# First attention phase: query/key parts and bf16 copies placed by DMA through DRAM instead of by selection matmuls and masked copies

## What is computed

```python
x = x + attn_a(layernorm(x))          # x: 16 sequences x 512 tokens x 256
qkv = xn @ w_qkv + b_qkv              # 16 heads of 16
scores = einsum('bhqd,bhkd->bhqk', q, k) * 16 ** -0.5
scores = where(mask, -inf, scores)    # heads 0-3: causal; heads 4-15: causal and a window of 64 keys
ctx = softmax(scores) @ v
x = x + ctx @ w_out + b_out
```

## Time and profile before

| | us |
|---|---|
| median of three executions | 3148.2 |
| profiled execution, span | 3151.3 |
| phase a, from the first instruction to its last store's issue | 1045.4 |
| busy in the whole span: PE, DVE, ACT, POOL | 2820.9, 2193.1, 1499.6, 1419.0 |

### The profile page before, as it was taken

How to read it: one execution, slowest core, us unless ns; L and a number is a source line. 1 busy time by engine, 2 the same in 40 slices (tenths; PEclk the granted TensorE clock), 3 DMA queues, 4 the chain that set the end, 5 groups by cost and what they waited for, 6 DMA issues and landing times. The chain is left out here.

```text
span 3151.3 us, 59461 instructions
## 1 busy us (share of the span) xinstructions
PE 2820.9 (90%) x17856; PEld 2175.0 (69%) x17856; DVE 2193.1 (70%) x5372; ACT 1499.6 (48%) x3002; POOL 1419.0 (45%) x1606
## 2 busy tenths in 40 slices
PE   6999999998999688898997999999999949999993
PEld 4565655565655457787896787778787739888872
DVE  8887787778886487765565676867777655566664
ACT  3455444454455234555775443344343317666651
POOL 1332233323333173446632533457575535655556
PEclk9999999999999788999998999999999979999996
DMA  4121111211211355657984222334343248888885
GB/s 151 48 89 49 49 55 70 68 49 56 73 58 49 134 190 178 220 195 268 324 291 145 86 76 71 99 112 127 111 127 105 96 156 300 289 304 302 299 277 155
DMA packets 208998, 465.15 MB, mean 148 GB/s; under 512 B 28448, under 2 KB 119712, under 8 KB 207648
## 3 DMA queue, kind: packets, MB, share of 16 engines
q1 hardware_dynamic: 159520, 326.86, 30.3%
q0 software_dynamic: 49152, 134.28, 12.8%
HBM read 217.24 MB, written 243.27 MB: 146 GB/s over the span
## 5 line engine op out<-in xcount | busy, mean ns | idle before, releaser
L381 POOL TENSOR_SCALAR_AFFINE_SELECT a_pt<-a_pt 128x512 f32<-128x512 f32 (+1 forms) x320 | 178.0, 556 | 669.5 <-ACT a_pt L481 668.8
L481 ACT ACTIVATE a_pt<-a_S 128x384 f32<-128x384 f32 (+3 forms) x640 | 254.6, 452 | 265.3 <-PE a_S L779 261.9
L1059 POOL DMA_INDIRECT slots<-f_xn,k_picks x256 | 260.0, 1016 | 254.2 <-PE f_Z L1567 99.7
L1842 POOL DMA_INDIRECT k_yg<-made,k_picks x224 | 223.6, 998 | 254.2 <-PE b_Y L2355 138.1
L2637 POOL DMA_INDIRECT f_yg<-made,k_picks x256 | 255.1, 997 | 170.8 <-PE f_Z L2830 89.7
L629 DVE TENSOR_REDUCE a_mx<-a_FB 128x2 f32<-128x384 f32 (+4 forms) x512 | 276.1, 591 | 26.7 <-PE a_FB L754 13.7
L751 PE MATMUL a_FB<-a_kb,a_qb 128*128 128x192 bf16 (+4 forms) x1024 | 206.1, 267 | 58.7 <-DVE a_mx L629 51.3
L1856 POOL DMA_INDIRECT slots<-b_staged,k_picks x160 | 162.3, 1015 | 105.9 <-issue 38.9
L792 PE MATMUL a_PV<-a_pt,a_vv 128*32 128x192 f32 (+4 forms) x2048 | 198.4, 371 | 2.7 <-POOL a_pt L388 2.6
L751 PEld LDWEIGHTS a_FB<-a_kb,a_qb 128*128 128x128 bf16 x1024 | 102.1, 100 | 135.1 <-DVE a_mx L629 87.0
L779 PE MATMUL a_S<-a_qs,a_ks 97*128 97x384 f32 (+3 forms) x640 | 178.3, 361 | 15.6 <-issue 15.3
(11 more groups left out here) (418 smaller groups left out, 7509.2 us busy)
## 6 DMA issues: line engine op xcount, KB each, us to landing
f_xg<-slots SPq DMA_DIRECT2D x164, 512.0 KB, 6.1
made<-f_ye SPq DMA_DIRECT2D x164, 512.0 KB, 4.0
slots<-a_zeros SPq DMA_DIRECT2D x16, 2560.0 KB, 9.2
a_xin<-in_x SPq DMA_DIRECT2D x16, 512.0 KB, 10.1
x_after_a<-a_xres SPq DMA_DIRECT2D x16, 512.0 KB, 2.9
f_wexp<-in_w_exp SPq DMA_DIRECT2D x8, 1024.0 KB, 13.4
k_xin<-bases SPq DMA_DIRECT2D x16, 512.0 KB, 5.7
x_after_b<-b_xres SPq DMA_DIRECT2D x16, 512.0 KB, 3.1
```

Source lines behind the costliest of these rows:

```text
L381: ins = nc.gpsimd.affine_select(out=v[:, :, 0:P], in_=v[:, :, 0:P], compare_op=ALU.is_ge, fill=0.0, base=0, pattern=[[0, nh], [1, P]], cha ...
L481: nc.scalar.activation(pt[:, u % 4, b * w:(b + 1) * w], S[:, s_bank[2 * u + b], 0:w], ACT.Exp).then_inc(e_done, 1)
L1059: nc.gpsimd.indirect_dma_start(out=slots[GROUP1[s]][:, :], out_offset=bass.IndirectOffsetOnAxis(ap=picks[:, i:i + 1], axis=0), in_=xn[:, s ...
L1842: nc.gpsimd.indirect_dma_start(out=yg[:, b, k, :], out_offset=None, in_=made[GROUP1[s]][:, :], in_offset=bass.IndirectOffsetOnAxis(ap=rout ...
```

## The change

The selection matrices, the rk and rq uses and the masks go. For each of two tiles t of 128 channels (8 heads), DVE makes bf16 copies `q16`, `k16` (`halve`, 4 casts of a sequence in slots 5 and 6). SP stores them to DRAM (`store_half`), waits until they have landed, and loads them back (`load_half`) with each head's 16 rows on partitions 0 to 15 of that head's place in `qb16` and `kb16`; the other partitions are zeroed once at the start. In the same way SP stores the four parts (`store_parts`) and loads them as nine DMAs for each t into `ks` and `qs` (`load_parts`). The factor 16^-0.5 moves into the exponential's scale. All front uses are now evicted by DVE in one count (`f_dve`), v and m move by a slot, mT by one, and `PE_FIRST` becomes (3, 4). The raw weights share memory with `pt`.

```diff
-    timed = ([(4, ("T", 0)), (4, ("T", 1)), (5, ("q", 0)), (6, ("k", 0)), (6, ("q", 1)), (6, ("k", 1)),
-              (10, ("v", 0)), (8, ("v", 1))] +
-             spread(9, 5.5, MAXG) + [(15, ("mT", 0))] + spread(13, 10.0, MAXL) + [(23, ("mT", 1))])
-    for p, slot in enumerate((15, 15, 16, 16, 18, 18, 21, 22)):
-        timed += [(slot, ("rk", p)), (slot, ("rq", p))]
+    timed = ([(4, ("T", 0)), (4, ("T", 1)), (5, ("q", 0)), (5, ("k", 0)), (6, ("q", 1)), (6, ("k", 1)),
+              (8, ("v", 0)), (9, ("v", 1))] +
+             spread(10, 6.0, MAXG) + [(16, ("mT", 0))] + spread(14, 10.0, MAXL) + [(24, ("mT", 1))])
...
-        PE_FIRST = (3, 7)
+        PE_FIRST = (3, 4)
-        MASK_AT = (5, 5, 8, 7)
-        K_AT = (6, 7)
+        HALF_AT = (5, 6)
...
+                def store_half(s, t):
+                    sp.wait_ge(halved, 2 * QT * s + 2 * (t + 1))
...
+                    for c, src in (("q", q16), ("k", k16)):
+                        sp.dma_start(half_d[c][s % 2, t * P:(t + 1) * P], src[:, t]).then_inc(half_stored[t], 16)
+
+                def load_half(s, t):
+                    sp.wait_ge(half_stored[t], 32 * (s + 1))
+                    if s:
+                        sp.wait_ge(f_done, ev(s - 1, NF, m_of[t]))
...
+                    for c, dst in (("q", qb16), ("k", kb16)):
+                        sp.dma_start(dst[0:DH, HT * t:HT * (t + 1), :],
+                                     half_d[c][s % 2, t * P:(t + 1) * P].rearrange("(h d) n -> d h n", d=DH)
+                                     ).then_inc(half_loaded[t], 16)
+
+                def store_parts(s, t):
+                    sp.wait_ge(f_dve, ev(s, NF, at["k", t]))
...
+                def load_parts(s, t):
+                    sp.wait_ge(parts_stored[t], 64 * (s + 1))
+                    if s:
+                        sp.wait_ge(s_done, ev(s - 1, 2 * NU, 2 * t_last[2 * t + 1] + 1))
...
+                    for n, i in enumerate((0, 0, 1)):
+                        sp.dma_start(ks[n * PAIR:(n + 1) * PAIR, PT * t:PT * (t + 1), :].bitcast(F32),
+                                     hilo_d["k"][s % 2, i, t * P:(t + 1) * P].rearrange("(a r) n -> r a n", r=PAIR)
+                                     ).then_inc(parts_loaded[t], 16)
+                    for n, i in enumerate((0, 1, 0)):
+                        for j in range(2):
+                            r = n * PAIR + j * DH
...
+                    if core:
+                        load_parts(s, 1)
                     if not isinstance(s, int) or 2 <= s + 2 < nseq:
                         load(s + 2, par)
                     if core:
                         m_rows(s, 1)
+                    if front:
+                        store_half(s + 1, 0)
+                        store_parts(s + 1, 0)
+                        store_half(s + 1, 1)
+                        load_half(s + 1, 0)
+                        store_parts(s + 1, 1)
+                        load_half(s + 1, 1)
                     if tail:
                         at_least(sp, t_dve, summed)
                         sp.dma_start(rows, xres[:, 1 - par]).then_inc(x_stored, 16)
                         at_least(sp, x_stored, stored)
                     if front:
+                        load_parts(s + 1, 0)
                         m_rows(s + 1, 0)
                         clear(s + 1)
...
-                def mask_q(s, four):
...
-                    for h in range(4 * four, 4 * four + 4):
-                        ins = nc.vector.tensor_scalar(qb16[:, h, :], qh[:, t, :].bitcast(F32),
-                                                      headmask[:, h % HT:h % HT + 1], None, ALU.mult)
...
+                def halve(s, t):
+                    at_least(dve, half_stored[t], ev(s - 1, 32, 31))
+                    for c, dst, src in (("q", q16, qh), ("k", k16, kh)):
+                        at_least(dve, hi_done, ev(s, NH, HIGH.index((c, t))))
+                        nc.vector.tensor_copy(dst[:, t, :], src[:, t, :].bitcast(F32)).then_inc(halved, 1)
...
+                nc.vector.memset(qs[0:ONES].bitcast(F32), 0.0).then_inc(dve_ready, 1)
...
-                    elif kind in ("rk", "rq"):
-                        c, t, a = kind[1], k // PT, k % PT
...
-                        pe.matmul(dst[0:ONES, :], sel[c + "h"][:, a].rearrange("p b c -> p (b c)"), hi[:, t, :],
-                                  start=True, stop=False)
-                        ins = pe.matmul(dst[0:ONES, :], sel[c + "l"][:, a].rearrange("p b c -> p (b c)"), lo[:, t, :],
-                                        start=False, stop=True)
                     elif kind == "m":
...
-                        at_least(pe, q_masked, ev(s, 4, heads[-1] // 4))
-                        at_least(pe, k_half, ev(s, QT, heads[-1] // HT))
+                        at_least(pe, half_loaded[heads[-1] // HT], ev(s, 32, 31))
```

More of the change, by code:

```diff
@@ L177, in phase_a @@
     s_bank, s_before = rotation(2 * NU, 3)
-    by_act = [kind == "rk" or (kind == "rq" and k in BY_ACT) for kind, k in FRONT]
-    act_no = [sum(by_act[:i]) for i in range(NF)]
-    dve_no = [i - act_no[i] for i in range(NF)]
-    NFA, NFD = sum(by_act), NF - sum(by_act)
     at = {use: i for i, use in enumerate(FRONT)}
     slot_front = {u: [i for i in range(NF) if timed[i][0] == u] for u in range(2 * NU)}
-    assert timed[-1][0] - NU < timed[0][0]
+    assert timed[-1][0] - NU <= timed[0][0]
     HIGH = [("T", 0), ("T", 1)] + [(c, t) for t in range(QT) for c in ("q", "k")]
@@ L242, in phase_a @@
         zeros = sb("zeros", [P, 4 * H])
+        hilo_d = {c: nc.dram_tensor("a_%s_parts" % c, (2, 2, H, SEQ), F32, kind="Internal").ap() for c in "qk"}
+        half_d = {c: nc.dram_tensor("a_%s_half" % c, (2, H, SEQ), BF16, kind="Internal").ap() for c in "qk"}
         S = ctx.enter_context(nc.psum_tensor("a_S", [P, 3, 512], F32))
@@ L263, in phase_a @@
         ch_done = sem("ch_done")
-        q_masked = sem("q_masked")
-        k_half = sem("k_half")
+        halved = sem("halved")
+        half_stored, half_loaded = ([sem("%s%d" % (n, t)) for t in range(QT)] for n in ("half_stored", "half_loaded"))
+        parts_stored, parts_loaded = ([sem("%s%d" % (n, t)) for t in range(QT)] for n in ("parts_stored", "parts_loaded"))
         m_row = sem("m_row")
@@ L293, in phase_a @@
         mt_at = [FRONT.index(("mT", g)) for g in range(2)]
+        m_of = [max(i for i in range(NF) if FRONT[i][0] == "m" and FRONT[i][1][0][-1] // HT == t) for t in range(QT)]
         with nc.Block() as block:
@@ L443, in front_use @@
                     kind, k = FRONT[i]
-                    if kind in ("T", "q", "k", "rk", "rq") and not (kind == "rq" and not by_act[i]):
+                    if kind in ("T", "q", "k"):
                         at_least(act, f_done, ev(s, NF, i))
@@ L452, in front_use @@
                         dst, b = (qh, bq) if kind == "q" else (kh, bk)
-                        at_least(act, f_done, ev(s - 1, NF, NF - 1))
+                        at_least(act, parts_stored[k], ev(s - 1, 64, 63))
+                        at_least(act, halved, ev(s - 1, 2 * QT, 2 * QT - 1))
                         nc.scalar.activation(dst[:, k, :], src, ACT.Identity, bias=b[:, k:k + 1]).then_inc(hi_done, 1)
-                    elif kind == "rk":
-                        at_least(act, s_done, ev(s - 1, 2 * NU, 2 * t_last[k // 2] + 1))
-                        nc.scalar.copy(ks[0:ONES, k, :], src[0:ONES]).then_inc(f_act, 1)
-                    elif kind == "rq" and by_act[i]:
-                        at_least(act, s_done, ev(s - 1, 2 * NU, 2 * t_last[k // 2] + 1))
-                        for j in range(2):
-                            ins = nc.scalar.activation(qs[0:ONES, 2 * k + j, :], src[0:ONES], ACT.Copy,
-                                                       scale=pairmask[0:ONES, j:j + 1])
-                        ins.then_inc(f_act, 1)
                 def log_variance(s):
@@ L481, in exps @@
                         nc.scalar.activation(pt[:, u % 4, b * w:(b + 1) * w], S[:, s_bank[2 * u + b], 0:w],
-                                             ACT.Exp).then_inc(e_done, 1)
+                                             ACT.Exp, scale=DH ** -0.5).then_inc(e_done, 1)
                 def pv_copy(s, t):
@@ L768, in scores @@
                     if u == t_first[t]:
-                        by = [i for i in range(NF) if FRONT[i][0] in ("rk", "rq") and FRONT[i][1] // 2 == t]
-                        at_least(pe, f_act, ev(s, NFA, act_no[[i for i in by if by_act[i]][-1]]))
-                        if not all(by_act[i] for i in by):
-                            at_least(pe, f_dve, ev(s, NFD, dve_no[[i for i in by if not by_act[i]][-1]]))
+                        at_least(pe, parts_loaded[t // 2], ev(s, 16 * PARTS, 16 * PARTS - 1))
                     for b in range(2):
@@ L842, in body @@
                             fronts()
-                pe.wait_ge(w_ready, 14)
+                pe.wait_ge(w_ready, NREADY)
                 iterations(pe, body)
```

111 lines of the change are left out of this document (40 added, 71 removed).

## The result

The change made the kernel slower: 3173.87 us, median of five executions (3157.66 to 3179.51), against 3148.2 (the median of five here too). The ratio is 1.0083, 95% interval [1.0058, 1.0107]. The forecast was 3037 us with a range from 2985 to 3102, so the result lies outside, on the other side. The profiled execution has a span of 3177.8 us.

A forecast was written before the change was run, and what follows sets the result against it. PE was taken as the bound, DVE close behind. Per sequence -11.3 + 2.7 + 1.0 = -7.6 us, times 15 is -114, with +3 for start and end: 3148.2 - 111 = 3037 us, range 2985 to 3102.

The forecast's parts named there:

- rk, rq, masks and the wait for maxima: Each sequence: PE matmuls 7.7 us, PE's long wait for a maximum 2.8 and low clock 0.8 removed, together 11.3 us.
- +2.7 for mT: Slot 4 of each sequence: PE waits 2.0 us for the last maxima before mT, and mT's copy on DVE adds 0.7.
- +1.0 for the halves: First m in slot 10: bf16 copies through DRAM arrive 0.1 to 3.3 us late; 1.0 us taken for each sequence.
- the 0.7 for mT's copy: DVE's order before the first q matmul: mT's copy delays it by 0.7 us, bounds 0 to 0.7.
- The bound of 1.5 us for short waits: Maxima stretch: a faster DVE could take up to 1.5 us out of PE's short waits; 0 was taken.
- Halves and parts: PE's waits for DRAM loads each sequence: halves 1.0 us late at the first m, parts in time at cost 0.
- the part on the parts through DRAM: SP is kept until about 17 us; parts arrive at 25 to 36, needed at 32: cost 0, bound 3.9 us.
- The clock: Low clock behind PE's wait for a maximum costs 1.7 us a sequence; 0.8 taken back, as similar new waits come.
- Start and sequence 0: First exponential -1 us (-6 to +6); m rows behind zeros at unit 8 of sequence 0 +6 us (0 to 14).
- Loads that come late (B): Loads onto few partitions are slow; parts 3.9 us late at unit 0, 3100 us in all; chance 0.15.
- work that was worth nothing (D): No change: DVE's removed work wasn't waited for and halves come 5 us late; chance 0.03.
- Rival C: Parts queued behind SP's wait for the output's store come 11.8 us late, +4.2 us a sequence, 3219 us; chance 0.07.

## Why the prediction was wrong

- *rk, rq, masks and the wait for maxima: right, somewhat low.* The terms came to -11.3 with +2.7 for mT and +1.0 for the halves. Measured where nothing else disturbs it (the last three periods with the residual moved): -10.5 instead of -7.6. The halves were in time, which is 1.0 of the 2.9, and the 0.7 for mT's copy doesn't show (the first product of the turned input waits 0.6 us in the whole phase). Most of the rest is the clock, of which 0.8 was counted. In a period outside the loop it was 0.97 before, which by an estimate from the row is 0.03 x 61.4 = 1.8 us, and is 1.00 now:

```profile
936.05:997.45 61.40, 57.14 (x441) 37.32 (x440) 50.26 (x105) 30.51 (x68) 20.57 (x34) 0.97 0.14 53
```

```profile
846.29:897.29 51.00, 47.50 (x408) 32.21 (x408) 34.60 (x80) 22.51 (x54) 20.06 (x33) 1.00 0.75 185
```

The bound of 1.5 us for short waits had no ground: the same sentence counts 0.6 for a sequence.

- *mT: right.* 1.8 us where 2.0 stood, again for a maximum.
- *Halves and parts: right in their own waits.* 0.4 and 1.5 us in all.
- *The step that failed* is the part on the parts through DRAM. It said that the stores of parts, second loads of halves and "the output's store, with SP's wait for its landing, keep SP until about 17 us", and used this only to ask when the parts are issued. It counted the output's store as something that occupies SP's order and never as something that is itself moved: 4.7 us later, landing 2.4 us more slowly, 6.2 us beyond GpSimd's need. The residual behind `x_stored` stands in the part of GpSimd's order that the change doesn't touch, and no row of before shows a wait there, because the store landed some 1.3 us before it was needed. Its lateness cost 83.8 us of waiting and 47 of PE's work at the lower clock; without it the time is 129 us less, of the 137 between 3037 and 3174. That 3045 then lies near 3037 is in part luck: outside the loop a sequence gains 10.5 us instead of 7.6, and the waits at the loop's turn bring the mean back to 7.0.
- *No term for the branch.* Issue of 2.8 to 3.5 us at the loop's turn was in the trace of before and taken as fixed. With the new traffic it is 6.5 to 7.3 us, and 1.4 to 4.6 more at the m of slot 1. In all it is worth 28 us (the parts) to 50 us (with the zeros).
- *The clock* was counted back with 0.8 us for a sequence, as if the new waits had the length of the old. A wait of 6.25 us was followed by some 6 us at 0.50.
- *Start and sequence 0: low, within their bounds.* First exponential +3.8 us where -1 stood, and 8.7 us at unit 8 where 6 stood. The first maximum comes at 45.26 instead of the 39 forecast: the first q starts 10.4 us later than before and not 5 (29.00 against 18.55), and the first m then waits 5.17 us for the halves. From there to the first exponential it takes 14.3 us, near the 15.5 forecast.
- *The rivals.* Loads that come late (B) are excluded by PE's waits of 0.4 and 1.5 us for them, and work that was worth nothing (D) by the 10.5 us. *Rival C* had the right family, "the queue becomes the bound", and the wrong victim: it made the last item in SP's order late (the parts) and let a rate decide. What was late was an old item in the middle, by the number of issues ahead of it. At 0.07 it had little weight for a change that puts 34 DMAs more for each sequence into one order.

These parts overlap: the two large ones are 129 and 28 to 50 us, against a better gain for each sequence and a miss of 137. The runs give each by itself and don't split the total without remainder.

## What to carry to other kernels

When DMAs are added to an engine's order, list every older DMA behind them, and for each who waits for its landing and with how much slack; a wait that the trace doesn't show is a slack, not an absence. Putting the older DMA first is no cure where it waits for its own data, since then the new ones wait with it: put each at the time at which its data is ready, or move the consumer. Judge a removed wait together with what was hidden behind it. A new wait can cost more than its length, through the clock behind it: here 83.8 us in waits of about 6 us each were worth 130.7, and the 20 us that an idle copy added at the loop's turn were worth 23.

## What the runs showed of the hardware

*Traffic and the branch.* PE's wait at the loop's turn that nothing in the profile ended was 2.8 to 3.5 us in a phase with a DMA share of 0.18, 7.3 us at the longest with parts and zeros under way, and 7.2 with an idle copy of 1.57 MB in DRAM.

*Loads onto few partitions.* While only parts are loaded (32 partitions at a time, then 16), the DMA engines are full at about half the rate that they reach in a stretch with the stores. Behind the wait shown above, with nine loads issued from 482.80 to 486.87, it is 186 GB/s at a share of 1.07 and then 142 at 1.03; the stretch with the stores:

```profile
470.00:475.00 5.00, 5.00 (x40) 4.08 (x39) 2.90 (x6) 2.05 (x7) 1.68 (x3) 1.00 0.95 324
```

That is 324 GB/s at a share of 0.95. The Trainium skill, page "SBUF — State Buffer", section "Door 1: The DMA port swizzle", gives 189 GB/s for partitions 0 to 31 and 104 for 0 to 15. The trace agrees in direction, with 186 near the larger figure and 142 between the two, though here several such loads to different partitions are in flight, and no run separates them.

*SP is held while much is queued.* In sequence 0, with 6144 KB and 2560 KB of zeros ahead of them, three issues took SP 12.20 us and six 8.29 us. Right behind the 2560 KB of a later sequence they took 2.90 and 5.32 us (from 503.50), and 1.25 and 2.78 with none ahead (from 482.80):

```profile
57.13 12.20 SPq L357 DMA_DIRECT2D a_ks<-a_k_parts  x3
69.37 8.29 SPq L363 DMA_DIRECT2D a_qs<-a_q_parts  x6
```

*DVE and GpSimd at the start.* The new memset of `kb16` on GpSimd ends at 19.52. DVE's operations on 128x4 elements, 0.16 us each before, took until 19.54:

```profile
15.67 3.87 DVE L579 TENSOR_SCALAR a_mean<-a_mean 128x4 f32<-128x4 f32 x1
```

```profile
12.60 6.92 POOL L475 MEMSET a_kb<- 128x8192 bf16 x1
```

The first transpose of the input starts 12.1 us later than before (24.79 against 12.65). Of that, 8.4 us were lost ahead of DVE's statistics (13.88 against 5.48), mostly by its memset of `qs` (6.88 us), and 3.7 here. The Trainium skill, page "SBUF — State Buffer", section "Who interferes with whom", calls the port pair that the two engines share an exclusive lock, held for a whole instruction; and names such operations of DVE with a scalar among those that can take it. A row that ends within 0.02 us of the memset is what that would leave; no run takes the memset away.
